# Turning an attention accumulator: block transposes by VectorE and 16 DMAs in place of TensorE transposes

## The reference

```python
xn = (x - mu) * rsqrt(var + 1e-5) * gamma + beta
q, k, v = split(einsum("bne,fe->bnf", xn, w_qkv), 3)      # 16 heads of 16
attn = softmax(where(causal, q @ k.T * 16 ** -0.5, -max))
x = layernorm(x + attn @ v)
h = silu(x @ w1.T * s1) * (x @ w2.T * s2)                 # 1024 wide
h = gelu(h @ h1.T * hs1); h = gelu(h @ h2.T * hs2)
out = layernorm(x + h @ w3.T * s3)
```

## Time and profile before

| | us |
|---|---|
| median of 3 runs | 2266.78 (2266.12 to 2267.12) |
| the profiled execution | 2266.53 |
| its span, first to last instruction | 2264.9 |
| attention stage, to TensorE's last first unit | about 1616 |
| mean granted clock of TensorE | 0.997 |

### The profile page before, as it was taken

One profiled execution on the slowest core, in us unless ns is written; L12 is line 12 of the kernel. 1 busy time (PEld: TensorE's weight loads), 2 busy tenths in 40 slices (PEclk: granted clock), 3 DMA queues, 4 the chain that ended last, 5 costly groups with the idle time before them and its releaser, 6 DMA issues. The chain is left out here.

```text
span 2264.9 us, 40406 instructions
## 1 busy us (share of the span) xinstructions
PE 2239.1 (99%) x15338; PEld 1244.2 (55%) x15338; DVE 1730.9 (76%) x3684; ACT 1623.4 (72%) x3087; POOL 228.3 (10%) x365
## 2 busy tenths in 40 slices
PE   8999999999999999999999999999999999999998
PEld 4444444444444445444444444443588888888887
DVE  8898998888999897888989898996535444544543
ACT  4677888899999898989989999999623433332332
POOL 3211110011110102111010211001100000000000
PEclk9999999999999999999999999999999999999999
DMA  3100001100000200000020000205500000000000
GB/s 103 34 24 17 4 20 41 38 20 20 20 20 1 59 20 20 20 20 20 1 57 20 20 20 20 78 1 168 186 10 17 3 19 19 11 9 19 16 4 20
DMA packets 72292, 70.17 MB, mean 31 GB/s; under 512 B 41632, under 2 KB 51744, under 8 KB 70688
## 3 DMA queue, kind: packets, MB, share of 16 engines
q1 hardware_dynamic: 67392, 56.03, 9.3%
q0 software_dynamic: 4704, 11.53, 1.7%
HBM read 28.20 MB, written 4.19 MB: 14 GB/s over the span
## 5 line engine op out<-in xcount | busy, mean ns | idle before, releaser
L741 ACT ACTIVATE PR<-bank 128x512 f32<-128x512 f32 (+1 forms) x2176 | 1092.6, 594 | 66.2 <-PE bank L1076 65.6
L831 DVE TENSOR_REDUCE pm<-bank 128x1 f32<-128x512 f32 x1422 | 920.3, 684 | 129.4 <-PE bank L1050 110.2
L1093 PE MATMUL bank<-PR,V 128*17 128x512 f32 (+3 forms) x4608 | 553.3, 562 | 0.5 <-POOL PR L623 0.4
L1491 PE MATMUL bank<-e_hid,e_h_sb 128*128 128x512 f32 x2048 | 466.2, 389 | 0.0
L1071 PE MATMUL bank<-MR,ones 64*128 64x512 bf16 (+3 forms) x2304 | 438.2, 369 | 1.2 <-DVE pm L834 0.7
L1491 PEld LDWEIGHTS bank<-e_hid,e_h_sb 128*128 128x128 f32 x2048 | 383.8, 188 | 81.2 <-DVE e_hid L1361 1.4
L1313 ACT ACTIVATE e_tmp<-bank,scales 128x512 f32<-128x512 f32 x128 | 88.3, 690 | 322.9 <-PE bank L1491 322.7
L726 ACT ACTIVATE mx_sb<-bank 128x512 f32<-128x512 f32 x370 | 221.3, 598 | 60.2 <-PE bank L1050 53.8
L834 DVE CUSTOM_DVE_ANT_0 bank<-bank,below 128x256 f32<-128x256 f32 (+3 forms) x512 | 239.8, 512 | 29.7 <-PE bank L1050 28.3
L1071 PEld LDWEIGHTS bank<-MR,ones 64*128 64x128 bf16 x2304 | 117.6, 93 | 250.9 <-issue 102.8
L826 DVE TENSOR_REDUCE pm<-mx_sb 128x1 f32<-128x512 f32 x370 | 250.0, 676 | 0.9 <-ACT mx_sb L726 0.8
(11 more groups left out here) (140 smaller groups left out, 1757.1 us busy)
## 6 DMA issues: line engine op xcount, KB each, us to landing
xnT<-in_h_dram SPq DMA_DIRECT2D x8, 1024.0 KB, 6.1
KA<-qk_hi SPq DMA_DIRECT2D x88, 64.0 KB, 2.2
KA<-qk_lo SPq DMA_DIRECT2D x88, 64.0 KB, 2.2
QX<-qk_hi SPq DMA_DIRECT2D x80, 64.0 KB, 2.2
QX<-qk_lo SPq DMA_DIRECT2D x80, 64.0 KB, 2.2
xres<-in_x_dram SPq DMA_DIRECT2D x8, 512.0 KB, 8.1
e_h_sb<-in_h_dram POOLq DMA_DIRECT2D x2, 2048.0 KB, 11.2
e_h_sb<-in_h_dram POOLq DMA_DIRECT2D x1, 4096.0 KB, 23.7
```

What stands on the lines that cost most here:

```text
L741: act.activation(PR[:, s % NPB, h, off:QB], ring_bank("score", s, h)[:, off:QB], ACT.Exp).then_inc(exp_done, 1)
L831: dve.reduce_max(pm[:, B % 2, i, a, p, 1 + c:2 + c], bank[:, :], AX.X).then_inc(mx_done, 1)
L1093: last = pe.matmul(ACC[32 * h:32 * h + VW, q:QB], V[:, v_tile(B, tile), GH * (B // NJ % 2) + h, :], PR[:, s % NPB, h, at:at + QB - q], sta ...
L1491: last = pe.matmul(RING[(4 + n) % NR][:, :], w[:, c, P * o:P * (o + 1)], hid[:, (T + layer) % 2, part, c, :], start=(c == 0 and part == 0) ...
```

## The change

ScalarE's two copies and TensorE's four transposes of a block go. In their place:

- `turn_sums` (VectorE) transposes ACC in 32x32 blocks from PSUM into acc_sb, where `copy_acc` stood, behind the block's last product. With heads on groups of 32 partitions this leaves head h's queries on the partitions 32h to 32h+31, query 128i + 32b + r on partition 32h + r, block (i, b).
- `invert_sums` (VectorE) at the end of the next block's first step (`move` in the list), on acc_sb.
- `scale_attention` (GpSimd), also at `move`, multiplies into attn_t. It waits until the move before has landed.
- `move_attention` (SyncE): 16 DMAs, one for each head h and partition block b, bring attn_t[32h.., b] to attn[32b.., h], 32 partitions x 256 bytes each. It waits for the addition of the block before.
- `attention_out` (GpSimd), five steps into the next block (`out`), waits for the 16 landings and adds to xres. Before, both stood one step ahead of the next block's end.
- `issue_order` merges moves and stacks into one list for SyncE: a move counts as two steps behind its place, a stack as one. The last move stands behind the weight test.
- COPIED loses the copies, so 392 maxima are relayed instead of 370, and ring banks are handed out anew.

```diff
--- before.py
+++ after.py
@@ -54,7 +54,8 @@
 NORM_AT, SPLIT_AT = 5, 14
 ROOT_BITS = float(0x5F3759DF)
 NEWTON = 3
-COPIED = ("norm", "qk", "v", "maxT", "acc", "acc_copy")
+COPIED = ("norm", "qk", "v", "maxT")
+ISSUED = {"move": 2, "qk": 1}
 INTRO_QK = 2
 SCALE_LEAD, NORM_LEAD = 4, 2
 
...
@@ -126,11 +127,8 @@
             if B // NJ % 2 == 0:
                 after.setdefault(START[B] - MAX_AHEAD, []).append(("v", v_unit(B)))
             last.setdefault(START[B] - MAX_AHEAD, []).append(("neg", B))
-            if B >= 2:
-                turns.setdefault(START[B] - MAX_AHEAD + 1, []).append(("acc", B - 2))
-                last.setdefault(START[B] - MAX_AHEAD + 2, []).append(("out", B - 2))
-        after.setdefault(START[NB - 1] + 1, []).append(("acc", NB - 2))
-        last.setdefault(START[NB - 1] + 2, []).append(("out", NB - 2))
+            last.setdefault(START[B], []).append(("move", B - 1))
+            last.setdefault(START[B] + 5, []).append(("out", B - 1))
         for s, (B, t) in enumerate(STEPS):
             self.ops += [("score", s, 0), ("score", s, 1)]
             units = []
...
@@ -149,10 +147,22 @@
             if (B, t) == (NB - 1, 4):
                 self.ops += [("x1",), ("test",)]
         self.ops += [("x1_turn",), ("av", len(STEPS) - 2), ("av", len(STEPS) - 1), ("acc_copy", NB - 1),
-                     ("first", 0), ("acc", NB - 1), ("out", NB - 1)]
+                     ("first", 0), ("move", NB - 1), ("out", NB - 1)]
         self.ops += [("first", n) for n in range(1, FIRST)]
         self.relays()
+        self.issue_order()
         self.count()
+
+    def issue_order(self):
+
+
+        step, found = 0, []
+        for op in self.ops:
+            if op[0] == "score":
+                step = op[1]
+            if op[0] in ISSUED:
+                found.append((step + ISSUED[op[0]], op))
+        self.issues = [op for _, op in sorted(found, key=lambda f: f[0])]
 
     def relays(self):
 
...
@@ -372,8 +382,9 @@
         mrest = sb("mrest", [P, TI, 2, 2])
         ident_r = sb("ident_r", [P, P], bf16)
         below = sb("below", [P, QB])
-        sums = sb("sums", [P, TI, GH, VW])
-        recip = sb("recip", [P, TI, GH, 1])
+        attn_t = sb("attn_t", [P, P // BLOCK, TI, D])
+        attn = sb("attn", [P, GH, TI, D])
+        recip = sb("recip", [P, TI, P // BLOCK, 1])
         qscale = sb("qscale", [P, 1])
         low_rows = sb("low_rows", [P, 2])
         pick = sb("pick", [P, 2])
...
@@ -488,6 +498,9 @@
 
         def stack_count(B):
             return 8 * 16 * qk_count(B)
+
+        def attn_count(B):
+            return 16 * GH * (P // BLOCK) * (B + 1)
 
         def xn_of(c):
             return xn_two[:, c - 1, :, :] if c in (1, 2) else xn_one[:, :, :]
...
@@ -550,11 +563,23 @@
                       .then_inc(wv_load, 16)
             load_weights(1)
             sp.dma_start(wvg[:, 1, :, :], wv[1, :, :].rearrange("p (c f) -> p c f", c=EC)).then_inc(wg_load[1], 16)
-            for B in range(NB):
-                if B >= INTRO_QK:
-                    stack(B)
-                if B % NJ == 0 and 0 < B < NB - NJ:
-                    load_weights(B // NJ + 1)
+            def move_attention(B):
+
+                sp.wait_ge(attn_done, B + 1)
+                if B >= 1:
+                    sp.wait_ge(res_done, B)
+                for h in range(GH):
+                    for b in range(P // BLOCK):
+                        sp.dma_start(attn[BLOCK * b:BLOCK * (b + 1), h, :, :],
+                                     attn_t[BLOCK * h:BLOCK * (h + 1), b, :, :]).then_inc(attn_moved, 16)
+
+            for op in PLAN.issues:
+                if op[0] == "move" and op[1] < NB - 1:
+                    move_attention(op[1])
+                if op[0] == "qk":
+                    stack(op[1])
+                    if op[1] % NJ == 0 and op[1] < NB - NJ:
+                        load_weights(op[1] // NJ + 1)
             sp.wait_ge(v_ready, NU)
             sp.wait_ge(qk_ready, qk_count(NB - 1))
             for v, scale in enumerate(ff_scales[0:4]):
...
@@ -570,6 +595,7 @@
                 sp.dma_start(chunks[n % 2], chunk).then_inc(chunk_load[n % 2], 16)
             sp.wait_ge(or_done, n_chunks + 2)
             sp.dma_start(low_row[:, :], low_part[:, :]).then_inc(row_load, 16)
+            move_attention(NB - 1)
             sp.wait_ge(scale_load, 16 * 5)
             sp.wait_ge(hi_stacked, stack_count(NB - 1))
             sp.wait_ge(lo_stacked, stack_count(NB - 1))
...
@@ -637,15 +663,19 @@
                 pool.wait_ge(mcol_part, 3 * B + 3)
                 pool.tensor_tensor(third, mrest[:, :, :, :], second, ALU.subtract).then_inc(mcol_done, 1)
 
+            def scale_attention(B):
+                pool.wait_ge(recip_done, B + 1)
+                if B >= 1:
+                    pool.wait_ge(attn_moved, attn_count(B - 1))
+                turned = acc_sb[:, :].rearrange("r (i b w) -> r b i w", i=TI, w=BLOCK)[:, :, :, 0:D]
+                by = recip[:, :, :, :].rearrange("r i b o -> r b i o").broadcast_to([P, P // BLOCK, TI, D])
+                pool.tensor_tensor(attn_t[:, :, :, :], turned, by, ALU.mult).then_inc(attn_done, 1)
+
             def attention_out(B):
                 g, j = divmod(B, NJ)
-                pool.wait_ge(recip_done, B + 1)
-                attn = sums[:, :, :, 0:D]
-                pool.tensor_tensor(attn, attn, recip[:, :, :, :].broadcast_to([P, TI, GH, D]), ALU.mult)\
-                    .then_inc(attn_done, 1)
-                pool.wait_ge(attn_done, B + 1)
-                own = xres[:, TI * j:TI * (j + 1), GE * g:GE * (g + 1)].rearrange("p i (h d) -> p i h d", h=GH)
-                pool.tensor_tensor(own, own, attn, ALU.add)\
+                pool.wait_ge(attn_moved, attn_count(B))
+                own = xres[:, TI * j:TI * (j + 1), GE * g:GE * (g + 1)].rearrange("p i (h d) -> p h i d", h=GH)
+                pool.tensor_tensor(own, own, attn[:, :, :, :], ALU.add)\
                     .then_inc(res_done, 1)
 
             for op in PLAN.ops:
...
@@ -657,6 +687,8 @@
                     normalise(op[1])
                 if op[0] == "neg":
                     split_maximum(op[1])
+                if op[0] == "move":
+                    scale_attention(op[1])
                 if op[0] == "out":
                     attention_out(op[1])
                 if op[0] == "score" and op[2] == 1:
...
@@ -740,21 +772,6 @@
                     act.wait_ge(st_ready, st_count(s, h))
                     act.activation(PR[:, s % NPB, h, off:QB], ring_bank("score", s, h)[:, off:QB],
                                    ACT.Exp).then_inc(exp_done, 1)
-
-            def copy_acc(B):
-                act.wait_ge(av_done, START[B + 1])
-                if B == 0:
-                    act.wait_ge(direct_done, 4 * INTRO_QK)
-                if B >= 1:
-                    act.wait_ge(at_ready, B)
-                act.activation(acc_sb[:, :], ACC[:, :], ACT.Copy).then_inc(acc_done, 1)
-
-            def copy_sums(B):
-                act.wait_ge(at_ready, B + 1)
-                if B >= 1:
-                    act.wait_ge(res_done, B)
-                turned = ring_bank("acc", B)[:, :].rearrange("p (i h w) -> p i h w", i=TI, h=GH)
-                act.activation(sums[:, :, :, :], turned[:, :, :, 0:VW], ACT.Copy).then_inc(sums_done, 1)
 
             act.wait_ge(consts, 1)
             act.activation(table[:, :], eps[:, :], ACT.Sqrt).then_inc(tabled, 1)
...
@@ -843,9 +856,18 @@
                 dve.tensor_reduce(rowmax[:, B % NX, :, :, :], pm[:, B % 2, :, :, :, 0:B % NJ + 1], axis=AX.X, op=ALU.max)\
                    .then_inc(rowmax_done, 1)
 
+            def turn_sums(B):
+                dve.wait_ge(av_done, START[B + 1])
+                if B == 0:
+                    dve.wait_ge(direct_done, 4 * INTRO_QK)
+                if B >= 1:
+                    dve.wait_ge(attn_done, B)
+                dve.transpose(acc_sb[:, :], ACC[:, :]).then_inc(acc_done, 1)
+
             def invert_sums(B):
-                dve.wait_ge(sums_done, B + 1)
-                dve.reciprocal(recip[:, :, :, :], sums[:, :, :, D:VW]).then_inc(recip_done, 1)
+                dve.wait_ge(acc_done, B + 1)
+                turned = acc_sb[:, :].rearrange("r (i b w) -> r i b w", i=TI, w=BLOCK)
+                dve.reciprocal(recip[:, :, :, :], turned[:, :, :, D:VW]).then_inc(recip_done, 1)
 
             def x1_statistics():
                 dve.wait_ge(res_done, NB - NJ + 1)
...
@@ -946,7 +968,9 @@
                     maximum(op[1], op[2])
                 if op[0] == "rowmax":
                     row_maximum(op[1])
-                if op[0] == "out":
+                if op[0] == "acc_copy":
+                    turn_sums(op[1])
+                if op[0] == "move":
                     invert_sums(op[1])
                 if op[0] == "test":
                     test_weights()
...
@@ -1119,14 +1141,6 @@
```

(8 more changed lines are left out.)

19 lines of the change are left out of this document (5 added, 14 removed).

## The result

The changed kernel takes **2290.8 us** (median of 4 runs, 2287.3 to 2293.5) where the kernel before takes 2267.0 beside it: a ratio of 1.0105, 95% interval 1.0087 to 1.0122. It is slower by 24 us, forecast were 15.5. The time lies inside the wide range of 2270 to 2292, at its upper end, and just outside the forecast's own range of 2276 to 2290.

What follows compares the result with a forecast made beforehand. TensorE was taken to set the pace up to the last block, ScalarE's exponentials in block 31. Terms -15.5 + 1 + 8.8 + 6.7 + 10.0 + 4.5 gave +15.5 us, 2282; own range 2276 to 2290, wide range 2270 to 2292.

Steps and rivals of the forecast that it cites:

- the VectorE rival: Full attention steps: no slack takes VectorE's added turn, so VectorE becomes the bound; +20 us more, 2302; chance 0.06.
- TensorE, -15.5: Attention stage: removing four transposes a block saves TensorE 0.50 us in each of 31 blocks, -15.5 us.
- ScalarE, 0: Attention stage: two copies a block removed from ScalarE, which does not end the steps outside block 31; priced at nothing.
- VectorE, +1: Attention stage: one added block transpose of 0.69 us a block, mostly in idle time; 0.03 a block, +1 us.
- Short blocks, +8.8: Moves 7, 8, 9 in a row and like places: TensorE stalls for GpSimd's late diagonal cut; +8.8 us, bounds 0 to 12.
- Weight test, +6.7: Last block: moves 29 and 30 hold SyncE ahead of the test's loads, so it ends late; +6.7 us exposed.
- Tail, +10.0: End of attention stage: the barrier waits for the last block's turn, scaling, 16 DMAs and addition; +10.0 us.
- Clock, +4.5: Start of feed-forward stage: after a pause of some 12 us TensorE runs 10.3 us at the low clock; +4.5 us.
- the clock holds: Rival at the barrier: pause not judged idle, or low stretch falls into it; sum +11, 2277.5 us; chance 0.15.
- Cheap issue: Rival on SyncE: 8 KB DMAs issue much faster, 0.3 us each, shrinking move and tail; -8, 2258 us; chance 0.04.
- The hidden test: Rival at the last block: moves 29 and 30 don't hold the weight test up; sum +9, 2275 us; chance 0.10.

Runs made afterwards that it cites:

- the kernel with two queues: Changed kernel with the last block's 16 transfers divided between SyncE and ScalarE, 8 each: 2282.3 us, ratio 1.0074.
- The last kernel: Changed kernel with weight-test loads first, every eighth block's addition later, GpSimd's maxima split before scaling, last block turned by TensorE as before: 2255.4 us, 0.9950.

## Why the prediction was right, and where its sizes were off

- **Direction and mechanism: right.** Slower (chance 0.87), by what it named: issue time in one queue, a cut queued behind a landing, a delayed weight test, a bare tail. That the time falls into the range is partly luck: the terms came out 8.8 us higher in sum than forecast, and the range reaches beyond 2290 only by a third of the VectorE rival, which fell.
- **TensorE, -15.5: mis-sized, the term that was furthest off.** The prediction's step is "They occupy 0.54 us" and from it "0.50 us a block". The step that held them is shorter by 0.44, but putting such transposes back costs 0.29 a block (8.6 us). The error is to take the spacing of instructions in a full timeline as what their removal brings: part of it comes back as a wait one step later. For what, the runs leave open; with the wait for ScalarE's copy of the maxima gone, the last step was no shorter.
- **ScalarE, 0, and VectorE, +1: small, as said,** but not measured apart. Without the transposes' share, the stalls and the waits for the maxima the change is worth -0.9 us in the steps, -4.2 in the last ones and +3.3 elsewhere. "ScalarE is not what ends the steps" is doubtful in one place: in block 12 the next block's first score started 0.15 us behind the end of its copy of the sums. In the ledger the steps that lost work give -10.0 where the first term has -15.5, and all other steps +0.4.
- **Short blocks, +8.8: mis-sized, measured 14.1.** The places, the chain and its cause are as said (moves landed at 503.9 and 516.8, forecast 505.1 and 517.8). The stalls came out at 8.5 us for the cut and 2.4 for the maxima, 10.9 together, since all three groups had them, block 18 with 1.9 and block 26 with 3.8. What was left out is the clock: waits of 2.6, 1.8 and 3.6 us lost another 1.1 us behind each. I had considered the clock only for the tail.
- **Weight test, +6.7: right,** 7.5 measured. The 1.2 us by which the slow cut lengthens a step of block 31 are hidden in it: TensorE's turn of x1 ends at 1614.3, 7 us ahead of the end of the test. With the loads first 8.6 us come back, since block 31's first two steps are 1.1 us shorter than before and the late test had hidden that too.
- **Tail, +10.0: right,** 10.1; 4.8 of it go with the second queue and all of it with the old way.
- **Clock, +4.5: mis-sized, 2.2 measured** from the restart on. The low stretch, taken as 10.3 us, had begun in the pause and lasted only 6 us behind the restart. So the rival's remark that it falls partly into the pause was half right.
- **Rivals.** That the clock holds fell (0.50 over 1640 to 1645 us). Cheap issue fell: 0.59 to 0.63 us each at 8 KB. VectorE as the bound fell: it is busy 76% as before, and TensorE's weight loads wait 191.3 us for its maxima where they waited 192.8. The hidden test fell.
- The sum's +15.5 is 24.3 in the trace: +5.5 by the steps that lost work, +5.3 by the short blocks, -0.6 by the rest, +0.8 by the test, +0.1 by the tail and -2.3 by the clock make up the 8.8 that are missing.

## What to carry to other kernels

Spreading a tile over partitions by DMA costs issue time per piece, 0.6 us here for 8, 16 and 64 KB alike (the 1 MB weight loads took 0.33), in the list of the engine that issues it; it is cheap in the middle of a long stage and bare at its end, so do the last tile in another way. When a late landing is added, look at what stands behind the waiting instruction in its engine's list: moving the addition two steps later in one block of eight was worth 12 us. And before counting an instruction's spacing as a gain, find the next wait of that engine; what precedes a wait is partly free.

## What the runs showed that I had not expected

- TensorE's granted clock fell to 0.5 (1.2 GHz) behind short waits in a stage in which it is otherwise full, and not behind each. In the changed kernel's trace it fell behind all three stalls (2.6, 1.8 and 3.6 us). In that of the kernel with two queues the waits were 2.6, 2.3 and 3.3 us, it fell behind the last alone, and the second steps of blocks 10 and 18 are 1.27 us shorter each. Without any move it fell behind two waits of 1.65 us; behind the barrier's 1.67 us it did not. The length of the wait alone doesn't decide it, and what does is open. The four runs of the kernel before lie within 1.1 us of each other, those of the changed one within 6.2. The last kernel, without these waits, lies within 1.2 again (2255.1 to 2256.2); that the low clock makes the spread is likely but was not separated.
- GpSimd's cut takes 1.87 us instead of 0.68 beside VectorE's ORs.
- Idle transposes on TensorE, put ahead of a wait, are about a third free: of 13.3 us, 7.5 came back in the next step, but 2.8 were lost again in the steps behind it.
